# Linear attention with a quantised layer beside it: scores in sixteen 32x32 tiles, shared PSUM banks, and V's rows through DRAM

## What is computed

```python
xn = layernorm(x)
# attention, 64 heads of 8
q, k, v = heads(xn @ Wq.T + bq), heads(xn @ Wk.T + bk), heads(xn @ Wv.T + bv)
q, k = softmax(exp(beta) * q), softmax(exp(beta) * k)      # over the 8 features of a head
kv  = cumsum(einsum('zsD,zsd->zsDd', k, v), axis=1)        # over the tokens
num = einsum('zsD,zsDd->zsd', q, kv)
den = sum(q * cumsum(k, axis=1))
attn = (num / den) @ Wo.T + bo
# beside it: xn rounded to fp8, times a weight matrix
ffn = fp8(xn / input_scale) * input_scale @ (weight_fp8 * weight_scale).T + bias
out = x + attn + ffn
```

## Time and profile before

| | us |
|---|---|
| median of 3 runs | 1174.45 (1173.78 to 1176.12) |
| profiled execution, its own time | 1173.3 |
| its span in the profile | 1171.5 |
| PE busy | 1117.6 |
| VectorE busy | 969.3 |
| ScalarE busy | 898.9 |
| GpSimd busy | 462.8 |

### The profile page before, as it was taken

The page is one execution under the profiler, slowest core; times in us unless marked ns, Lnnn a source line. Parts: engine busy times, 40 slices in busy tenths (PEclk is TensorE's granted clock), DMA queues, the critical chain, the costliest instruction groups (busy, mean ns, idle before and its releaser), DMA issues.

```text
span 1171.5 us, 57412 instructions
## 1 busy us (share of the span) xinstructions
PE 1117.6 (95%) x24103; PEld 629.9 (54%) x24103; DVE 969.3 (83%) x1975; ACT 898.9 (77%) x1933; POOL 462.8 (40%) x714
## 2 busy tenths in 40 slices
PE   1589999999999999999999999999999999999996
PEld 1345555555555555555555555555555555555553
DVE  5688888888888888888888888888888888888883
ACT  1377887878878787887878788887878888787873
POOL 3234344344434434443443444344344434434420
PEclk9789999999999999999999999999999999999999
DMA  9223353345345544553554455345444333344331
GB/s 243 42 59 82 89 83 93 93 85 87 95 87 83 97 92 82 87 97 85 83 96 89 87 89 95 87 83 98 91 84 87 95 87 84 98 90 85 70 77 49
DMA packets 156469, 104.39 MB, mean 89 GB/s; under 512 B 111969, under 2 KB 128481, under 8 KB 156257
## 3 DMA queue, kind: packets, MB, share of 16 engines
q1 hardware_dynamic: 155536, 99.76, 42.3%
q10 hardware_dynamic: 720, 1.31, 0.3%
HBM read 40.20 MB, written 16.78 MB: 49 GB/s over the span
## 4 chain that ended last, share of the span: by engine, by line
PE 93%; DMA 2%; DVE 2%; ACT 1%; issue 1%; SPq 0%; POOL 0%; ACTq 0%; DVEq 0%
PE s_ps L948 11%; PE a_ps L1052 7%; PE k_ps L914 5%; PE vo_ps L914 5%; PE k_ps L1008 5%; PE k_ps L916 5%; PE k_ps L918 5%; PE k_ps L925 5%; PE k_ps L927 5%; PE k_ps L929 5%; PE q_ps L916 5%; PE vo_ps L918 5%; PE q_ps L918 5%; PE vo_ps L916 5%; PE q_ps L914 5%; PE a_ps L1037 4%
## 5 line engine op out<-in xcount | busy, mean ns | idle before, releaser
L488 ACT ACTIVATE st_pairs<-st_run 32x144 f32<-32x144 f32 x1008 | 331.0, 328 | 11.9
L424 POOL TENSOR_TENSOR w_own<-vp,cst 128x576 f32<-128x576 f32 x126 | 142.1, 1149 | 323.3 <-DVE vp L746 323.3
L548 ACT ACTIVATE q_heads<-qT,cst 128x512 f32<-128x512 f32 x256 | 163.9, 711 | 4.8 <-DVE qT L762 3.8
L690 DVE TENSOR_TENSOR att<-s_ps,cst 128x512 f32<-128x512 f32 x256 | 163.5, 680 | 0.0
L411 POOL TENSOR_TENSOR y_sum<-y,y_magic 128x512 f32<-128x512 f32 x64 | 81.5, 1274 | 153.4 <-DVE y_magic L648 153.4
L948 PE MATMUL s_ps<-q_heads,w_own 64*64 64x128 f32 x4096 | 141.3, 275 | 0.3 <-DVE att L690 0.3
L948 PEld LDWEIGHTS s_ps<-q_heads,w_own 64*64 64x64 f32 x4096 | 110.4, 132 | 54.0 <-issue 53.9
L530 ACT ACTIVATE w_own<-kT,cst 128x512 f32<-128x512 f32 x128 | 85.4, 714 | 62.3 <-DVE kT L730 62.3
L404 POOL TENSOR_TENSOR x_split<-xn,x_split 128x512 f16<-128x512 f32 x64 | 74.7, 1167 | 138.8 <-ACT x_split L471 138.8
L471 ACT ACTIVATE x_split<-xn 128x512 f16<-128x512 f32 x64 | 40.3, 630 | 94.3 <-DVE xn L637 94.3
L914 PE MATMUL k_ps<-w_hi,xT 128*128 128x512 f16 x256 | 98.6, 385 | 5.0 <-ACT k_ps L587 2.6
(11 more groups left out here) (152 smaller groups left out, 2277.2 us busy)
## 6 DMA issues: line engine op xcount, KB each, us to landing
v_groups<-vp SPq DMA_DIRECT2D x512, 36.0 KB, 3.2
x_in<-L_attn_x SPq DMA_DIRECT2D x64, 256.0 KB
x_res<-L_attn_x SPq DMA_DIRECT2D x64, 256.0 KB
out<-o_sb SPq DMA_DIRECT2D x64, 256.0 KB
w_own<-L_attn_Wk SPq DMA_DIRECT2D x1, 1024.0 KB, 12.6
w_own<-L_attn_Wq SPq DMA_DIRECT2D x1, 1024.0 KB, 14.6
w_own<-L_attn_Wv SPq DMA_DIRECT2D x1, 1024.0 KB, 16.4
att<-L_ffn_weight_fp SPq DMA_DIRECT2D x1, 1024.0 KB, 18.0
```

The lines of the kernel that those rows point to most:

```text
L424: last = gp.tensor_tensor(v_pairs[:, c].rearrange("p h w -> p (h w)"), vp[:, t.parity].rearrange("p h w -> p (h w)"), pair_mask[:, c:c + 1 ...
L488: last = sc.activation(st_pairs[TOK * b:TOK * (b + 1), to, u::J, :, b % SP, :], st_run[TOK * u:TOK * (u + 1), b // SP, :, b % SP, :, :], A ...
L548: last = sc.activation(q_heads[:, i.parity, :, j, :], qT[:, i.parity, :, :], ACT.Copy, scale=head_mask[:, j:j + 1])
L690: v.tensor_tensor(att[:, c % 2, 4 * (c // 2):4 * (c // 2) + 4, :, :] .rearrange("p g j s -> p (g j) s"), s_ps[:, DM * (c % 2):DM * (c % 2 ...
```

## The change

The scores of a half become 32 matmuls in sixteen tiles of 32x32, each with one sequence's rows and one class of 16 heads. The four sequences write to four banks, and the order turns so that four matmuls in a row touch four rows of tiles and four columns. The keys need no masked copies, so `k_pairs` and ScalarE's work on it go, and k's transpose is double buffered. For the four banks of scores, V and Q share `q_ps` (V waits until Q has been shifted; Q's seed waits until V has been scaled), and the transposes go to `k_ps` (after K has been shifted; the seed for the output products waits for the low part). `split_low` moves ahead of the variances. V's rows are written to DRAM by one DMA and read back by four, one for each class, which stand behind the two transposes on the queue. `intra` goes by pairs of sequences in place of halves of the heads, and its first part runs ahead of V.

```diff
-            def move_v(t):
+            def write_v(t):
                 sp.wait_ge(vp_ready, (t + 1).n)
                 if t.after(2):
+                    sp.wait_ge(v_moved[t.parity], t.half * 16 * CL)
+                sp.dma_start(v_rows[t.parity].rearrange("b s h w -> (b s) h w"), vp[:, t.parity])\
+                    .then_inc(v_written[t.parity], 16)
+
+            def read_v(t):
+                sp.wait_ge(v_written[t.parity], (t + 2).half * 16)
+                if t.after(2):
                     sp.wait_ge(a_done, (t - 1).n)
-                for b in range(SEQS):
-                    for gp in range(GP):
-                        to = SP * gp + b % SP
-                        sp.dma_start(v_groups[TOK * to:TOK * (to + 1), t.parity, to, b // SP],
-                                     vp[TOK * b:TOK * (b + 1), t.parity, HEADS // GP * gp:HEADS // GP * (gp + 1)])\
-                            .then_inc(v_moved[t.parity][b], 16)
+                for c in range(CL):
+                    sp.dma_start(v_groups[TOK * c:TOK * (c + 1), t.parity, c],
+                                 v_rows[t.parity, :, :, J * J * c:J * J * (c + 1)].rearrange("b s h w -> s b h w"))\
+                        .then_inc(v_moved[t.parity], 16)
...
                 if (i - 1).exists():
-                    move_v(i - 1)
+                    write_v(i - 1)
                 if (i + 1).exists():
                     turn_x(i + 1)
                 if i.exists():
                     turn_xq(i)
+                if (i - 1).exists():
+                    read_v(i - 1)
...
# ScalarE
+                if i.exists() and i.after(1):
+                    act.wait_ge(vp_ready, i.n)
+                    sc.activation(q_ps[:, :], bias[:, MQ, :], ACT.Copy).then_inc(qseed_ready, 1)
...
+                    act.wait_ge(aT_done, (d + 1).n)
+                    sc.activation(flat(ah[:, :, :]), k_ps[:, :], ACT.Copy).then_inc(ah_ready, 1)
+                    act.wait_ge(al_ready, (d + 1).n)
                     sc.activation(k_ps[:, :], bias[:, 3, :], ACT.Copy, scale=out_up[:, :])\
                         .then_inc(oseed_ready, 1)
...
-                    for c in range(SP):
-                        last = sc.activation(k_pairs[:, i.parity, :, c, :], kT[:, :, :], ACT.Copy,
-                                             scale=pair_mask[:, c:c + 1])
...
# PE
-                for q in range(4):
-                    for gp in range(GP):
-                        g = GP * (4 * half + q) + gp
-                        for n in range(SEQS // SP):
-                            rows = slice(SP * TOK * n, SP * TOK * (n + 1))
-                            last = mm(s_ps[SP * TOK * gp:SP * TOK * (gp + 1), DM * n + P * q:DM * n + P * (q + 1)],
-                                      k_pairs[rows, t.parity, g, :, :].rearrange("p c s -> p (c s)"),
+                for u in range(2 * half, 2 * half + 2):
+                    for turn_ in range(CL):
+                        for b in range(SEQS):
+                            c = (b + turn_) % CL
+                            g = class_group(c, u)
+                            rows = slice(TOK * b, TOK * (b + 1))
+                            last = mm(s_banks[TOK * c:TOK * (c + 1), b, u, :], kT[rows, t.parity, g, :],
                                       q_heads[rows, t.parity, g, :, :], start=True, stop=True)
...
-                if i.after(1):
-                    pe.wait_ge(vp_ready, i.n)
-                project(vo_ps, i, MV, seeded=False).then_inc(v_done, 1)
+                pe.wait_ge(qshift_ready, (i + 1).n)
+                project(q_ps, i, MV, seeded=False).then_inc(v_done, 1)
...
# turn_attention
+                if (t + 2).exists():
+                    pe.wait_ge(kshift_ready, (t + 3).n)
...
-            def intra(t, h):
+            def intra(t, n):
-                pe.wait_ge(att_ready, t.n * 4 + 2 * h + 2)
+                pe.wait_ge(att_ready, (t + 1).n * 4)
...
+                for b in range(SP * n, SP * n + SP):
+                    cols = slice(VW * (b % SP), VW * (b % SP + 1))
                     for j in range(J):
                         for u in range(J):
+                            last = mm(a_rows[TOK * u:TOK * (u + 1), b // SP, :, :, j, cols]
+                                      .rearrange("p h l w -> p l h w"),
+                                      att[:, b, u, j, :], v_groups[:, t.parity, :, b, J * u + j, :],
+                                      start=False, stop=True, skip_group_check=True)
...
                 if t.exists():
                     inter(t, i.exists())
+                    intra(t, 0)
                 if i.exists():
                     values(i, fold)
                 if t.exists():
-                    intra(t, 0)
                     intra(t, 1)
```

More of the change, by code:

```diff
@@ L42 @@
 G = HEADS // J
+CL = G // J
 KC = DM // P
@@ L262, in build @@
         qheads_ready, v_cleared, st_cleared = sem("qheads_ready"), sem("v_cleared"), sem("st_cleared")
-        kpairs_ready, vpairs_ready = sem("kpairs_ready"), sem("vpairs_ready")
-        v_moved = [[sem(f"v_moved{n}_{b}") for b in range(SEQS)] for n in range(2)]
+        vpairs_ready = sem("vpairs_ready")
+        v_written = [sem("v_written0"), sem("v_written1")]
+        v_moved = [sem("v_moved0"), sem("v_moved1")]
         scores_done, att_ready = sem("scores_done"), sem("att_ready")
@@ L525, in body @@
                 if i.exists():
-                    act.wait_ge(kT_ready, (i + 1).n)
-                    if i.after(2):
-                        act.wait_ge(scores_done, (i - 1).n * 2)
-                    for c in range(SP):
-                        last = sc.activation(k_pairs[:, i.parity, :, c, :], kT[:, :, :], ACT.Copy,
-                                             scale=pair_mask[:, c:c + 1])
-                    last.then_inc(kpairs_ready, 1)
                     act.wait_ge(qshift_ready, (i + 1).n)
@@ L722, in key_sums @@
                     dve.wait_ge(state_done, (i - 1).n)
-                    for b in range(SEQS):
-                        dve.wait_ge(v_moved[i.parity][b], i.half * 16 * GP)
+                    dve.wait_ge(v_written[i.parity], i.half * 16)
                 v.reciprocal(vp[:, i.parity, :, DH].rearrange("p (l q j) -> p q l j", l=GP, j=J),
@@ L727, in key_sums @@
                     .then_inc(krec_ready, 1)
-                if i.after(1):
-                    dve.wait_ge(kpairs_ready, i.n)
-                v.transpose(kT[:, :, :].rearrange("p g s -> p (g s)"), k_e[:, i.parity, :])\
+                if i.after(2):
+                    dve.wait_ge(scores_done, (i - 1).n * 2)
+                v.transpose(kT[:, i.parity].rearrange("p g s -> p (g s)"), k_e[:, i.parity, :])\
                     .then_inc(kT_ready, 1)
@@ L1040, in inter @@
                                    start=(h == 0 and gp == 0), stop=False, skip_group_check=True)
-            def intra(t, h):
-                pe.wait_ge(att_ready, t.n * 4 + 2 * h + 2)
-                if h == 0:
-                    for b in range(SEQS):
-                        pe.wait_ge(v_moved[t.parity][b], (t + 2).half * 16 * GP)
-                    pe.sem_inc(pe_waited, 1)
-                for n in range(SEQS // SP):
+            def intra(t, n):
+                pe.wait_ge(att_ready, (t + 1).n * 4)
+                if n == 0:
+                    pe.wait_ge(v_moved[t.parity], (t + 2).half * 16 * CL)
+                pe.sem_inc(pe_waited, 1)
+                for b in range(SP * n, SP * n + SP):
+                    cols = slice(VW * (b % SP), VW * (b % SP + 1))
                     for j in range(J):
                         for u in range(J):
-                            last = mm(a_rows[TOK * u:TOK * (u + 1), n, h, :, j, :],
-                                      att[:, n, J * h + u, j, :],
-                                      v_groups[:, t.parity, :, n, J * h + u, j, :], start=False, stop=True,
-                                      skip_group_check=True)
-                if h == 1:
+                            last = mm(a_rows[TOK * u:TOK * (u + 1), b // SP, :, :, j, cols]
+                                      .rearrange("p h l w -> p l h w"),
+                                      att[:, b, u, j, :], v_groups[:, t.parity, :, b, J * u + j, :],
+                                      start=False, stop=True, skip_group_check=True)
+                if n == 1:
                     last.then_inc(a_done, 1)
@@ L1070, in body @@
                     pe.wait_ge(bias_ready, 3)
+                    pe.wait_ge(kshift_ready, (i + 1).n)
                     for j in range(J):
-                        last = transpose(t_ps[:, P * j:P * (j + 1)],
-                                         bv_sorted[:, P * j:P * (j + 1)],
-                                         ident)
+                        last = mm(k_ps[:, P * j:P * (j + 1)], bv_sorted[:, P * j:P * (j + 1)], ident,
+                                  start=(j == 0), stop=(j == J - 1), is_transpose=True, skip_group_check=True)
```

(3 more changed lines are left out.)

82 lines of the change are left out of this document (38 added, 44 removed).

## The result

The changed kernel takes **1204.31 us** (median of 4 runs, 1203.27 to 1204.83) where the kernel before takes 1174.55 (median of its 4): 1.0251 times as long, 95% interval 1.0233 to 1.0268. The forecast was 1174.0 with 1162 to 1200 around it; the time lies above the range. The profiled run took 1203.27 us, its span is 1201.3.

A forecast was written before the change was run, and what follows sets the result against it. TensorE was taken to bound the kernel, 17.07 us a step. Steps of 17.00 us gave -4.7 us over 62 steps, single costs +4.2: -0.5 in sum, carried over to 1174.0 us, range 1162 to 1200.

The forecast's parts named there:

- The scores, the step that failed: Each half of the scores on TensorE in sixteen 32x32 tiles: 0.85 us in place of 1.04, saving 0.19 us.
- late: One step in four, where VectorE ends its shift and masks later; transposes wait until 4.84 us, next step at 17.32 us.
- rival C: Finer tiles bring the scores nothing, 1.04 us a half; steps of 17.21 and 17.50 us, kernel 1192 us; chance 0.08.
- Single costs: Costs outside the steady steps, in step 1 and the run's last steps: together +4.2 us.
- The fold: Step 1's folding product goes into Q's bank and waits for the shift of Q: about +2.3 us.
- The last two steps' chain through the seed: At the run's end, high part, low part, seed, quantised product lie bare: about +1.4 us, and +0.5 one step earlier.
- L: Time for the reads of V's rows from DRAM to land before intra's first part: taken as 2.8 us.
- rival B: V's rows land late for intra, from a landing time of 3.0 us; 1186 us at 3.2, 1198 at 3.4; chance 0.28.
- the extra change of tiles: Intra's part ahead of V adds one change of tile shape on TensorE per step: 0.14 us.
- the seed chain: Transposes, high part, low part, seeding: seeded about 7.7 us into the step, quantised product wants it at 8.4; costs nothing.
- rival D: Intra's output in four runs of 9 values doubles each pass's time: +54 us, kernel 1229 us; chance 0.04.
- one rate: Intra's cut runs and the state share's single run of 72 fit the same price, 6.9 ns a pass.

## Right and wrong, by the prediction's steps

- **The scores, the step that failed: "I take 0.85".** Measured 1.00. The prediction took the bursts of 64 passes (0.82) as its model and added a little, but those stream 72 columns a pass and these 128 (with 64 columns the half does take 0.79). The array's part, 0.109 for each of four rounds, and the price of 32 more records, 0.38 to 0.40, add up, and 0.85 had the records at the price of a narrower burst. So the saving is 0.04 a half and not 0.19. The first half's 0.15 was partly under the shift of K (transposes at K+4.51 instead of 4.41), the second half's is open: intra's first part at K+13.06 instead of 12.81, late 13.41 instead of 13.24. Times 45 and 15 steps 17.16 - 16.89 and 17.51 - 17.32: **15 us** over the forecast. In its effect this is rival C (17.21 and 17.50), which had 0.08.
- **Pauses.** No step of the prediction has them: 7.4 us in the steps. It took for granted that a PE timeline without waits stays so when short bursts stand closer together.
- **Single costs.** The fold was right (+2.7 with a pause of 0.8 in it, forecast +2.2). Step 0 was missed: V's product there waits for the shift of Q, 3.4 us by the waits view, since V now goes to Q's bank; +2.6. The last two steps' chain through the seed was taken at +1.9; the end is +7.7, V's rows and pauses included.
- **V's rows.** Right in the steps, but with little room: the last read lands at K+11.2 to K+12.9, 0.2 to 2.0 us ahead of intra's first part, and nothing waits. L was 2.1 in place of 2.8 (median), and rival B fails there. At the end, where PE comes early, the same path is bare: 2.28 us. The prediction weighed reads and their landing; the slow part is the write.
- **Right in the sum, by luck in the term:** 0.14 was taken for the extra change of tiles and 0.16 measured for intra as a whole, but the change is 0.09 of it and the new cut of the same 128 records 0.07.
- **Right:** transposes at K+4.84 in late steps (4.89) with the shift of K as their wait; the seed chain free in the steps; the next K 4.08 after intra's first part (4.10); rival D. The Trainium skill (PSUM — Partial Sum Buffer, Specifications (TRN2)) has non-contiguous patterns slow a matmul significantly. This trace does not agree: 64 passes with four runs of nine take 0.70, and the state's share, 64 passes with one run of 72, takes 0.82. The prediction's "one rate" was itself drawn through two rows and could not test it.

**Open:** why the packets of instructions start late at some places and not at others. With V's write from ScalarE and intra behind V no pause is left in the steps 2 to 61, with the statistics later three, while each of the first two edits alone leaves 7 to 10 us. At eight places where intra behind V by itself has a pause, the packet starts 1.0 to 2.0 us ahead of the last record before it; with both edits it starts 3.1 to 3.5 us ahead. What brings it forward was not tested. The clock's fall at the end was read, not tested on its own: the last quantised product (four matmuls, 1.03 us before) took 1.86 or 1.87 in every version of the changed kernel but the one with the statistics later (1.02).

## What to carry to other kernels

Count the instructions of a burst as well as its columns: a cut into more tiles pays only while the rounds saved (0.109 us each here) outweigh the extra records (6 to 12 ns each beyond the first 32 here), and the nearest burst of another width is no model for it. Look where the blocks of instructions change when short bursts stand close together: 7.4 us of the changed kernel's steps were lost there without a semaphore. Read the end of the run by itself: a path with 0.2 to 2.0 us to spare in each step stands bare there. And look which DMA engines a transfer uses: loads of 256 KB with an outermost dimension of four ran as if on four of sixteen, an unrelated write of 18 KB took 6.4 us beside them, and splitting it was worth 6 us to the old kernel, 13 to the new.

## Unexpected of the hardware

- The first 32 short records of a burst start 6.7 ns apart, the later ones one or two per 17 ns, with 128 columns and with 32.
- A write's time to landing did not depend on its bytes (6.4 us for 18 KB, 6.8 for 288 KB) nor much on its queue (5.8), but on the other transfers (2.3 to 3.0 once those were given out in four).
- TensorE can stand 0.3 to 4 us, once 5.8, inside a burst with no semaphore behind it, and 64 tiny matmuls far ahead of it move the place by a step. All 222 such pauses here stand at the same place of a block of 256 instructions, and none is passed less than 2.1 us after the 16 KB packet of instructions of the same number started.
